# Cross attention and a mixture of experts on one core: Silu moved forward, tile table and expert pieces moved back, and another ending

## The reference

```python
x = x + xattn(layernorm(x), k, skip, ctx, ctx, 8)      # x, ctx: 8 x 256 x 512, float32
x = x + ffn(layernorm(x), gate_w, shared and expert weights)

# ffn, for xf: 2048 tokens x 512
scores = sigmoid(xf @ gate_w.T)                        # 8 experts
topk_w, topk_idx = top_k(scores, 2)
topk_w = 2.5 * topk_w / topk_w.sum()
shared = silu(xf @ shared_wg.T) * (xf @ shared_wu.T) @ shared_wd.T        # width 704
h = silu(xf @ exp_wg.T) * (xf @ exp_wu.T)              # width 352, for each expert
routed = sum over a token's two experts of topk_w * (h @ exp_wd.T)
out = shared + routed
```

## Time and profile before

| | |
|---|---|
| median of 3 runs | 715.76 us (710.89 to 716.21) |
| profiled execution | 713.33 us, span 711.6 us |
| busy: PE | 654.1 us (92%) |
| busy: DVE | 445.0 us (63%) |
| busy: POOL | 352.1 us (49%) |
| busy: ACT | 293.9 us (41%) |
| mean granted clock of PE | 0.978 of full speed |
| moved by DMA | 91.57 MB |
| last group's shared blocks, PE | 428 to 459 us |
| tiles, PE | 474 to 702 us |

### The profile page before, as it was taken

One profiled execution on the slowest core, in us unless ns is written; L12 is line 12 of the kernel. 1 busy time (PEld: TensorE's weight loads), 2 busy tenths in 40 slices (PEclk: granted clock), 3 DMA queues, 4 the chain that ended last, 5 costly groups with the idle time before them and its releaser, 6 DMA issues.

```text
span 711.6 us, 11541 instructions
## 1 busy us (share of the span) xinstructions
PE 654.1 (92%) x3475; PEld 330.6 (46%) x3476; DVE 445.0 (63%) x720; ACT 293.9 (41%) x374; POOL 352.1 (49%) x294
## 2 busy tenths in 40 slices
PE   5979878977999989899999999899799999999993
PEld 3534334433444445344444434345455555555551
DVE  4999988886987695998796787873432211221110
ACT  4356579333233553223531277623433332333321
POOL 2999899926676354694566006400132223222322
PEclk8899999999899999999999999999999999999998
DMA  7944326012234700223313668967998888988954
GB/s 196 288 119 110 99 88 146 20 46 55 106 104 91 177 28 18 90 76 63 86 30 120 240 197 288 318 191 184 226 148 144 130 124 137 132 130 127 141 74 59
DMA packets 130519, 91.57 MB, mean 129 GB/s; under 512 B 96992, under 2 KB 110816, under 8 KB 129952
## 3 DMA queue, kind: packets, MB, share of 16 engines
q1 hardware_dynamic: 121728, 71.49, 41.3%
q0 software_dynamic: 8176, 18.75, 15.0%
q10 hardware_dynamic: 576, 0.82, 0.5%
HBM read 46.32 MB, written 25.65 MB: 101 GB/s over the span
## 4 chain that ended last, share of the span: by engine, by line
PE 55%; DVE 16%; POOL 10%; ACT 9%; DMA 4%; issue 4%; SPq 1%; POOLq 0%; DVEq 0%; ACTq 0%
PE banks L808 16%; PE banks L810 16%; PE banks L809 16%; POOL arena L654 7%; DVE mixT L1460 2%; PE banks L900 2%; DVE arena L1453 2%; DVE stats L1466 2%; PE banks L904 1%; PE banks L905 1%; POOL arena L711 1%; DMA arena<-split_filters 1%; DVE hm L1607 1%; POOL arena L682 1%; DVE silu L1495 1%
## 5 line engine op out<-in xcount | busy, mean ns | idle before, releaser
L654 POOL TENSOR_TENSOR arena<-arena 128x512 f32<-128x512 f32 x120 | 140.4, 1200 | 58.7 <-ACT arena L1153 31.5
L771 POOL DMA_INDIRECT out<-xf,ids x39 | 60.8, 1560 | 184.7 <-DMA out<-xf,ids 145.5
L808 PE MATMUL banks<-arena 128*128 128x512 f16 (+1 forms) x330 | 124.3, 377 | 17.0 <-DVE arena L1453 13.4
L809 PE MATMUL banks<-arena 128*128 128x512 f16 (+1 forms) x330 | 124.4, 377 | 0.0
L810 PE MATMUL banks<-arena 128*128 128x512 f16 (+1 forms) x330 | 124.3, 377 | 0.0
L808 PE MATMUL banks<-arena,normed 128*128 x312 | 97.7, 313 | 0.0
L809 PE MATMUL banks<-arena,normed 128*128 x312 | 97.7, 313 | 0.0
L810 PE MATMUL banks<-arena,normed 128*128 x312 | 97.6, 313 | 0.0
L1825 DVE SCALAR_TENSOR_TENSOR hm<-banks,silu 128x256 f32<-128x256 f32 x39 | 16.6, 424 | 116.9 <-PE banks L810 116.9
L1113 ACT ACTIVATE arena<-arena 128x2048 f16<-128x2048 f32 x31 | 59.0, 1904 | 71.4 <-POOL arena L654 68.7
L1453 DVE TENSOR_TENSOR arena<-banks,arena 128x512 f32<-128x512 f32 x128 | 80.4, 682 | 11.7 <-PE banks L810 11.4
(11 more groups left out here) (193 smaller groups left out, 1078.5 us busy)
## 6 DMA issues: line engine op xcount, KB each, us to landing
arena<-split_filters SPq DMA_DIRECT2D x31, 256.0 KB, 3.4
arena<-in_expert_w SPq DMA_DIRECT2D x12, 544.0 KB, 8.5
stages<-in_expert_w SPq DMA_DIRECT2D x10, 544.0 KB, 6.2
arena<-in_ctx_hidden SPq DMA_DIRECT2D x4, 1024.0 KB, 8.1
arena<-in_ctx SPq DMA_DIRECT2D x8, 512.0 KB, 6.4
out<-x_tok SPq DMA_DIRECT2D x6, 512.0 KB, 5.3
x_tok<-in_expert_w SPq DMA_DIRECT2D x5, 544.0 KB, 7.0
mixT<-in_expert_w SPq DMA_DIRECT2D x5, 544.0 KB, 7.8
```

The costliest lines, as they stand in the source:

```text
L654: nc.gpsimd.tensor_tensor(kv[s % 2][:, lb * COLS:(lb + 1) * COLS].rearrange("p (b j i) -> p b j i", i=NH, j=NH), v[:, a, None, :].to_broad ...
L771: nc.gpsimd.indirect_dma_start(out=out, out_offset=bass.IndirectOffsetOnAxis(ap=ids[slot][:, 0:1], axis=0), in_=yg[slot], in_offset=None, ...
L808: nc.tensor.matmul(dst, wh, xh, start=(k == 0), stop=False)
L809: nc.tensor.matmul(dst, wh, xl, start=False, stop=False)
```

## The change

- ACT does the Silu of block 1 of the last group ahead of its four operations on pieces 2 and 3 of expert 2. The pieces of experts 3 and 4 move one block later on ACT (expert 4's last two come after the blocks), and those of expert 3 one block later on DVE.
- `tile_table` runs behind block 4's low half on DVE, a block later, and has three more operations. They make `last_own`: how many additions of its own parity the last tile's addition must wait for, one fewer than all where tiles 36, 37 and 38 are one expert's.
- SP issues pieces 2 and 3 of expert 6 at tiles 2 and 3 (both were issued at tile 1) and the pieces of expert 7 at tiles 4 to 7 (they were at 2 to 5). ACT and DVE split them behind tiles 3 and 4, and 5 to 8 (they were 2 and 3, and 4 to 7). The pieces 0 and 1 of expert 6 stay where they were.
- The down products of tiles 37 and 38 go to banks 7 and 6 and don't wait for bank 4. The last addition has a semaphore of its own, and in all additions GpSimd's wait for the output comes behind the waits for the other additions.

```diff
@@ out_bank, used by tile_down and tile_out
+        def out_bank(t):
+            return bank[4 + (2 + t % 2 if isinstance(t, int) and t >= TILES - TURNED_LAST else 0)]
@@ pieces_behind
-        pieces_behind = {1: [(6, 0), (6, 1)], 2: [(6, 2)], 3: [(6, 3)]} | {c + 4: [(7, c)] for c in range(EX_PARTS)}
+        pieces_behind = {1: [(6, 0), (6, 1)], 3: [(6, 2)], 4: [(6, 3)]} | {c + 5: [(7, c)] for c in range(EX_PARTS)}
@@ SyncE
                 if t == 1:
                     sp.wait_ge(base_ready, Q * G)
                     store(out_rows[G - 1], x_tok[(G - 1) % 3], base_stored)
-                    load_expert(6, 2, 3)
                 elif t >= RING:
                     sp.wait_ge(added[t % 2], 16 * (t // 2 - 1))
                     load_ids(t, t % RING)
-                if 2 <= t < 2 + EX_PARTS:
-                    load_expert(E - 1, t - 2)
+                if 2 <= t < RING:
+                    load_expert(6, t)
+                elif t >= RING:
+                    load_expert(E - 1, t - RING)
...
-                sp.wait_ge(added[i], 16 * len(range(i, TILES, 2)))
+                sp.wait_ge(added[i], 16 * len(range(i, TILES - 1, 2)))
+            sp.wait_ge(last_added, 16)
@@ GpSimd
-            def add_tile(t, slot, own, other):
-                pool.wait_ge(r_y, t + 1)
+            def add_tile(t, slot, own, other, done=None):
                 if other is not None:
                     pool.wait_ge(added[1 - slot % 2], other)
                 pool.sem_inc(pool_passed, 1)
                 if own is not None:
                     pool.wait_ge(added[slot % 2], own)
+                pool.wait_ge(r_y, t + 1)
...
-                    in_=yg[slot], in_offset=None, compute_op=ALU.add).then_inc(added[slot % 2], 16)
+                    in_=yg[slot], in_offset=None, compute_op=ALU.add).then_inc(done or added[slot % 2], 16)
...
-            for t in range(TILES - 2, TILES):
-                add_tile(t, t % RING, 16 * (t // 2), before_of(t))
+            add_tile(TILES - 2, (TILES - 2) % RING, 16 * ((TILES - 2) // 2), before_of(TILES - 2))
+            own = pool.value_load(last_own[0:1, 0:1], min_val=16, max_val=16 * TILES)
+            add_tile(TILES - 1, (TILES - 1) % RING, own, before_of(TILES - 1), last_added)
@@ TensorE, tile_down
-                if not isinstance(t, int) or t > 0:
+                if not isinstance(t, int) or 0 < t < TILES - TURNED_LAST:
                     pe.wait_ge(r_y, t)
...
-                    bank[4],
+                    out_bank(t),
@@ ScalarE, last group
             gated(G - 1, 0, gates[0])
-            expert_for_pool(pool_expert, 2)
-            expert_for_pool(pool_expert, 3)
             for m in range(1, SM):
                 gated_silu(G - 1, m, gates[m % 2])
-                if m < SM - 1:
-                    expert(3 + (m - 1) // 2, 2 * (m - 1) % EX_PARTS)
+                if m == 1:
+                    expert_for_pool(pool_expert, 2)
+                    expert_for_pool(pool_expert, 3)
+                elif m < SM - 1:
+                    expert(3 + (m - 2) // 2, 2 * (m - 2) % EX_PARTS)
                 gated_high(G - 1, m)
-                if m < SM - 1:
-                    expert(3 + (m - 1) // 2, 2 * (m - 1) % EX_PARTS + 1)
+                if 1 < m < SM - 1:
+                    expert(3 + (m - 2) // 2, 2 * (m - 2) % EX_PARTS + 1)
+            expert(4, *second_half)
             expert(5)
@@ VectorE, tile_table
-                link(nc.vector.tensor_scalar(tile_prev[:], t_start, 16.0, None, ALU.mult))
+                all_landed = float(16 * ((TILES - 1) // 2))
+                link(nc.vector.tensor_scalar(tile_prev[:], t_start, 16.0, None, ALU.mult),
+                     nc.vector.tensor_scalar(last_two[:], t_start[:, TILES - 2:TILES], -1.0, float((TILES - 1) // 2),
+                                             ALU.mult, ALU.add))
+                link(nc.vector.tensor_tensor(last_own[:], last_two[:, 0:1], last_two[:, 1:2], ALU.mult))
+                link(nc.vector.tensor_scalar(last_own[:], last_own[:], -16.0, all_landed, ALU.mult, ALU.add))
@@ VectorE, last group
-                if m < 3:
-                    expert(3, 2 * m - 2)
+                if 1 < m < 4:
+                    expert(3, 2 * m - 4)
                 gated_low(G - 1, m)
-                if m < 3:
-                    expert(3, 2 * m - 1)
-                elif m == 3:
+                if 1 < m < 4:
+                    expert(3, 2 * m - 3)
+                elif m == 4:
                     tile_table()
```

More of the change, by code:

```diff
@@ L195, in xattn_moe @@
         tile_prev = sb("tile_prev", [1, SLOTS], I32)
+        last_two = sb("last_two", [1, 2], I32)
+        last_own = sb("last_own", [1, 1], I32)
         turned_rows = xf.rearrange("p t a c -> p (t a c)").bitcast(F32)
@@ L246, in xattn_moe @@
         added = [sem(f"added{i}") for i in range(2)]
+        last_added = sem("last_added")
         kv_ready = sem("kv_ready")
@@ L1337, in tile_out @@
                     act.wait_ge(added[slot % 2], 16 * ((RING // 2) * (n - 2) + slot // 2 + 1))
-                nc.scalar.activation(yg[slot], bank[4], ACT.Copy, scale=ids[slot][:, 1:2].bitcast(F32)
+                nc.scalar.activation(yg[slot], out_bank(t), ACT.Copy, scale=ids[slot][:, 1:2].bitcast(F32)
                                      ).then_inc(r_y, 1)
```

## The result

The changed kernel took 719.95 us (median of 15 runs, 717.32 to 722.96), the kernel before, run beside it, 715.45 (15 runs, 710.89 to 718.43). The ratio is 1.0067, with a 95% interval of 1.0047 to 1.0088: slower by 4.8 us. The profiled execution took 720.06 us, with a span of 718.0 and a mean granted clock of 0.973.

A forecast was written before the change was run, and what follows sets the result against it. TensorE (PE) was taken as the bound, so only holes in its work count. Terms -1.4 - 5.1 + 6.4 + 1.7 - 1.8 = -0.2 us gave 713.1 for the profiled execution, 715.5 on the runs' level; range 708 to 720.

The forecast's parts named there:

- slow rival: Tile 7's piece issued at 524.1, landing in 7.6 us, tile 9 starting at 534.3: +4.8 us, 720.5; chance 0.12.
- Part 2: First tiles: one piece per tile on SyncE removes the wait for tile 2's transpose and its low clock, gaining 5.1 us.
- Part 3: Before tile 9: the later last piece opens a hole of some 6 us, costing 6.4 plus 1.7 us for the clock.
- Which chain: SyncE at tile 7: the last piece waits for tile 3's addition to land at 519.8 and is issued at 521.4.
- a remark in the slow rival: Late pieces before tile 9: each also holds ACT, hence the next hidden rows; no size of its own.
- Behind the wait: Tile 9's start: PE goes on 0.1 us after VectorE's low half of the last piece.
- The landing: Last piece of expert 7: lands 5.3 us after its issue.
- Part 1: Last group's blocks: earlier Silu, later table; first two holes go, one to 462.4 opens in the down product; gain 1.4 us.
- Part 4: Ending: down products 37 and 38 back to back, last addition issued at 701.4 to 702.1; gain 1.8 us.
- The short hole: Before tile 9: only the 3.2 us of ACT and VectorE, without low clock: -5.1 us, 710.4; chance 0.2.
- 707.2: Rival of no hole before tile 9, if another wait covers it: -8.3 us; chance 0.05.
- The rule quoted against the move: For the pieces' later loads: issue a DMA early, compute, wait late; by it alone, the slow rival's time.

The follow-up runs named there:

- e12: Kernel before with only one piece per tile on SyncE, conversion two tiles behind issue, PE asking only for its own expert's pieces up to tile 12: 0.9924, -5.4 us.
- e1: Kernel before with only the changed ending (banks of down products 37 and 38, last addition's semaphore and count, GpSimd's wait order): 0.9993, -0.5 us.
- e2: Kernel before with only the last group's change (Silu of block 1 first, pieces and table a block later): 0.9994, -0.4 us.
- e10: Kernel before with PE's tiles 9 to 12 written out, each waiting only for its own expert's pieces: 1.0023, +1.6 us.
- e6: e4 with ACT and DVE converting pieces two tiles behind their issue, tiles 9 to 12 written out there too: 0.9907 of the kernel before, -6.7 us.
- e8: Changed kernel with SyncE issuing expert 7's pieces right behind the row load, ahead of the hidden transpose: 1.0033 of the kernel before, +2.4 us.
- e11: e4 with tiles 9 to 12 again waiting for all 28 pieces, tile 9's weight place in a register before the wait: 1.0054 of kernel before, +3.9 us.
- e9: e6 without the last group's part, so Silu, pieces and table in their old order: 0.9907 of the kernel before, -6.7 us.
- e4: Changed kernel, PE's tiles 9 to 12 each waiting only for their own expert's pieces, all 28 before tile 13: 0.9964 of the kernel before, -2.6 us.
- e3: Kernel before with only the pieces' change: one piece per tile on SyncE, conversion a tile later: 1.0099, +7.1 us.
- e5: Changed kernel with the tile table behind block 5 in place of block 4: 1.0055 of the kernel before, +3.9 us.

## Why the prediction was wrong

The forecast was -0.2 us and it was +4.8: wrong in sign, on the side and by the size of the slow rival, in the place where that rival stood. By its parts:

- **Part 2 was right.** 5.1 us were forecast up to tile 4 and 5.0 are found up to the end of tile 6's down product (a new hole of 0.75 us before tile 5's included); tile 2's wait and the low clock behind it are gone, and the mended part alone (e12) gives 5.4. That the size fits so well is partly luck: in the four traces with the old loads (the kernel before, e1, e2, e10) tile 2's wait is 2.9 to 5.2 us, with the low clock behind it in three.
- **Part 3 is where the sum failed.** The hole came where it was forecast and behind the last piece, but the step to that piece's issue, by the landing of tile 3's addition, was wrong, and with it the size. I wrote 6.4 for the hole and 1.7 for the clock. The table has 10.4 and 1.3: 3.6 too little. Tile 9 was forecast for 529.3, which is 530.7 with the 1.4 us by which this execution ran late, and started at 536.39. That start, 5.7 us late, is the miss (5.0 in all, with 0.4 less for the clock). The hole is only 4.0 us longer than forecast, since PE came to it 1.7 us later than forecast. Three terms make up the 5.7: the issue 3.8, the way from issue to low half 0.2, what follows the low half 1.6.
  - *Which chain.* I put the piece behind tile 3's addition, issued at 521.4, which is 522.8 in this execution. It was issued at 526.6. The addition had landed by then, at 523.5; it had been issued behind ACT's output of its tile, not behind another addition's landing. What was missing is that each late piece also stands before ACT, and that SyncE's own order comes behind that. I had that only as a remark in the slow rival. e6 shows it: with ACT never standing, the same program of SyncE issues the piece 2.6 us sooner, counted from tile 0. e8, which issues it 3.9 us sooner, shows that SyncE's order has a share as well.
  - *Behind the wait.* 1.73 us of loop start and register load came after the wait; I had put 0.1 there without a reason. e11 took them away in the trace.
  - *The landing* was 5.6, as said (5.3). The slow rival's 7.6 us weren't needed for its result.
- **Part 1 was right in its holes and wrong in its gain.** The holes before blocks 3 and 4 went, and one of 2.07 us appeared where I had put 2.3. But I left out the clock there, which I had priced two parts further on: 464 to 467 ran at 0.50, which costs about 1.6 us and leaves +0.1 for -1.4. It wasn't a price of the change in every execution: the old order had its hole at the same place (1.6 to 2.3 us) and the low clock behind it in two of six profiles, the new order in all six with the table behind block 4. e2 and e9 say that the part is worth nothing in time.
- **Part 4 was right in the trace** (-1.9 for -1.8; the last tiles are one expert's), and not shown by the runs of e1 (-0.5, between -1.9 and +0.9). That the gain is real is argued from the traces only.
- **The rivals.** The short hole didn't come, since the piece came late. (Two of the rivals' times were counted from the forecast's 715.5 in place of the 715.8 before: 710.4 should be 710.7, and 707.2 should be 707.5. Nothing hangs on it.) The slow rival had 0.12 and its time, 720.5, is nearly the measured one, but partly by luck: its addition landing at 522.5 and its 7.6 us of landing aren't what happened, while the remark that a late piece holds ACT, given no price there, is. With four tiles of pieces landing before a waiting ACT, that remark should have been the forecast.
- The rule quoted against the move, from the Trainium skill's "DMA: Bandwidth & Descriptors" (Rules for kernel authors), has two halves, and the runs bear out the second: e4 and e6 leave the issue where the change put it and only wait later, and gain 7.4 and 11.5 us over the changed kernel.

Not tried: a run of e6 with the old issue of pieces on SyncE, which would tell how much of its gain is owed to the conversion alone. e10 and e12 don't settle it. The trace of the kernel before speaks for little: ACT stands before one of the six pieces there (6.91 us, behind tile 2) and takes the other five with no wait.

## What to carry to other kernels

When a load moves later, move with it everything that waits for it, the conversion and the consumer's wait, and look first at whether the consumer needs it there at all: a wait for "all pieces" placed where a loop begins opened a hole of 10 us, 7.4 us of the time, for pieces that the next four tiles mostly don't need. On an engine that works in order, a wait for a late transfer is paid by everything queued behind it, and through that by the queue that issues the next transfer, so price a chain of such pieces as a loop and not as a single landing. And a hole that the change leaves behind has to be priced with the clock at every place, not only at the largest.

## What the runs showed of the hardware

Whether TensorE's clock falls behind a short hole isn't settled by the hole's length here. In e2 the first of these rows has 1.66 us of idle and the low level in the 3 us behind it (mean 0.68), the second 2.85 us of idle and full clock:

```profile
463.74 0.39 PE L900 MATMUL banks<-arena,hTh 128*128 128x512 f16 x1 [1.66 <-DVE hTl L1617]
...
503.62 0.39 PE L808 MATMUL banks<-arena,mixT 128*128 x1 [2.85 <-DMA mixT<-x_tok]
```

```profile
464.00:467.00 3.00, 3.00 (x10) 0.99 (x9) 3.00 (x4) 0.95 (x1) 0.00 (x0) 0.68 0.91 341
...
503.00:506.00 3.00, 2.38 (x12) 1.26 (x13) 2.21 (x4) 0.86 (x3) 1.05 (x1) 1.00 1.18 356
```

In e3 a hole of 1.85 us at the first one's place had full clock behind it. So a hole of about 2 us costs either itself or itself and some 1.6 us more.

Behind the hole of 5.20 us in e10 and each of the five of 8.4 us and more the level was 1.2 GHz, and its price varied. Tile 9's gate and up products, up to tile 7's down product, take 3.58 us at full clock (529.42 to 533.00 in the kernel before). Behind the hole they took 4.87 in the changed kernel, 4.88 in e5, 5.33 in e3, 5.96 in e8 and 6.44 in e11: 1.3 to 2.9 us more. A gain of a microsecond or two in such a hole can be hidden by that.
